# Both scatter-adds of an expert block issued together, with a set of padding rows for each

## The reference

```python
probs = softmax(xt @ Wr + br)
top_p, top_idx = top_k(probs, 2)
weights = top_p / top_p.sum(axis=-1, keepdims=True)
xn = (xt - mu) * rsqrt(var + 1e-5)
xe = xn[None] * ln_g[:, None] + ln_b[:, None]           # 8 experts
h = gelu(einsum('end,edh->enh', xe, W1) + b1)           # 256 -> 1024
y = einsum('enh,ehd->end', h, W2) + b2                  # 1024 -> 256
out = (weights[:, :, None] * y[top_idx]).sum(axis=1)    # added to x
```

## Time and profile before

| | us |
|---|---|
| median of 3 runs | 4400.84 |
| lowest, highest | 4399.68, 4402.47 |
| span of the profiled execution | 4400.9 |
| experts stage (about) | 3390 to 4400.9 |

### The profile page before, as it was taken

One profiled execution on the slowest core, in us unless ns is written; L12 is line 12 of the kernel. 1 busy time (PEld: TensorE's weight loads), 2 busy tenths in 40 slices (PEclk: granted clock), 3 DMA queues, 4 the chain that ended last, 5 costly groups with the idle time before them and its releaser, 6 DMA issues. The chain is left out here.

```text
span 4400.9 us, 84837 instructions
## 1 busy us (share of the span) xinstructions
PE 4086.7 (93%) x19450; PEld 3374.9 (77%) x19450; DVE 2987.8 (68%) x5419; ACT 2610.6 (59%) x8831; POOL 2599.1 (59%) x2378
## 2 busy tenths in 40 slices
PE   4999599999999999999999999999985888888887
PEld 3888488888888888888888888888985777777776
DVE  5666699999999999999999999997666000000000
ACT  1444587888788878887888787776232222222222
POOL 3444577777777777777777777775113233333332
PEclk8999799999999999999999999999967999999999
DMA  3333333443444333433443444433223455555554
GB/s 117 103 101 98 116 103 103 104 104 103 104 104 104 104 104 104 103 103 104 104 104 103 103 103 104 104 103 85 79 80 107 147 153 152 155 161 156 152 161 119
DMA packets 432067, 497.39 MB, mean 113 GB/s; under 512 B 253111, under 2 KB 343707, under 8 KB 417707
## 3 DMA queue, kind: packets, MB, share of 16 engines
q0 software_dynamic: 105984, 260.17, 22.1%
q1 hardware_dynamic: 326059, 236.92, 18.8%
HBM read 433.72 MB, written 63.07 MB: 113 GB/s over the span
## 5 line engine op out<-in xcount | busy, mean ns | idle before, releaser
L615 POOL DMA_INDIRECT k_x<-gather_table,edges_src x1760 | 1995.9, 1134 | 576.9 <-issue 446.4
L632 ACT ACTIVATE k_x<-k_x,edges_y 128x64 f32<-128x64 f32 x5280 | 1303.0, 335 | 4.9 <-DMA k_x<-gather_table,edges_src 4.9
L738 PE MATMUL edges_ps_sum<-k_x,edges_hot_y 128*128 128x256 f32 x3520 | 1094.2, 393 | 0.5 <-issue 0.5
L738 PE MATMUL edges_ps_sum<-k_x,edges_hot 128*128 128x256 f32 x3520 | 1048.1, 379 | 0.0
L639 ACT ACTIVATE edges_hot_y<-edges_hot,edges_y 128x128 f32<-128x128 f32 x1760 | 562.4, 390 | 506.9 <-DVE edges_hot L678 506.9
L727 PE MATMUL edges_ps_edge<-k_w_e,edges_hT 100*128 100x256 f32 x3520 | 836.4, 380 | 7.8 <-ACT edges_hT L625 7.8
L694 DVE TENSOR_TENSOR k_x<-k_x,edges_ps_edge 128x768 f32<-128x768 f32 x880 | 794.4, 941 | 0.0
L738 PEld LDWEIGHTS edges_ps_sum<-k_x,edges_hot_y 128*128 128x128 f32 x3520 | 633.6, 190 | 175.3 <-issue 107.1
L727 PEld LDWEIGHTS edges_ps_edge<-k_w_e,edges_hT 100*128 100x128 f32 x3520 | 670.8, 191 | 101.5 <-issue 7.6
L738 PEld LDWEIGHTS edges_ps_sum<-k_x,edges_hot 128*128 128x128 f32 x3520 | 670.0, 190 | 91.1
L1341 DVE TENSOR_TENSOR experts_raw<-experts_ps_y,experts_b 128x256 f32<-128x256 f32 x112 | 42.3, 419 | 908.7 <-PE experts_ps_y L1297 908.7
(11 more groups left out here) (233 smaller groups left out, 3996.6 us busy)
## 6 DMA issues: line engine op xcount, KB each, us to landing
experts_w<-in_w SPq DMA_DIRECT2D x112, 1024.0 KB
k_x<-gather_table,edges_src POOLq DMA_INDIRECT x1760
edges_el<-el_hi SPq DMA_DIRECT2D x880, 20.0 KB
edges_el<-el_lo SPq DMA_DIRECT2D x440, 20.0 KB
nodes_el<-in_el SPq DMA_DIRECT2D x46, 170.0 KB, 2.4
el_hi<-nodes_el_hi SPq DMA_DIRECT2D x46, 170.0 KB, 1.9
el_lo<-nodes_el_lo SPq DMA_DIRECT2D x46, 170.0 KB, 2.0
experts_b<-in_b SPq DMA_DIRECT2D x56, 128.0 KB
```

Of the source, the lines that this page charges most:

```text
L615: nc.gpsimd.indirect_dma_start(out=rows[k][:, j, :], out_offset=None, in_=K.table_d.rearrange("t p d -> (t p) d"), in_offset=bass.Indirect ...
L632: x = nc.scalar.activation(Z[k % 2][:, j, MUL * (i + 1):MUL * (i + 2)], rows[k][:, j, 0:MUL], ACT.Identity, scale=y[k][:, j, 1 + i:2 + i])
L738: x = t.matmul(into[:, :, o, :], rows_hot[k % 2][:, j, :], msg[k % 2][:, j, o * D:(o + 1) * D], start=j == 0 and o == 0, stop=j == GC - 1, ...
```

## The change

The second scatter-add of a block no longer waits for the first. Both wait once for the two of the block before. As both halves of one block can then be under way together, the halves get different padding rows: `spare` has two columns, N_PAD + 1 + p and N_PAD + 129 + p, and `out` and `tok_d` have one more tile of 128 zero rows, which SP writes in the update stage.

```diff
-            sp.dma_start(out[NT], K.zeros[:, 0:D]).then_inc(c["begun"], 16)
-            sp.dma_start(K.tok_d[NT], K.zeros[:, 0:D]).then_inc(c["begun"], 16)
+            for pad in (NT, NT + 1):
+                sp.dma_start(out[pad], K.zeros[:, 0:D]).then_inc(c["begun"], 16)
+                sp.dma_start(K.tok_d[pad], K.zeros[:, 0:D]).then_inc(c["begun"], 16)
...
-            sp.wait_ge(c["begun"], 48)
+            sp.wait_ge(c["begun"], 80)
...
-            done(v.tensor_scalar(empty[:, :], empty[:, :], spare[:, :], None, ALU.mult))
+            by_half = empty[:, :].rearrange("p (b s) -> p b s", s=2)
+            done(v.tensor_tensor(by_half, by_half, spare[:, :].unsqueeze(1).to_broadcast([P, C // 2, 2]), ALU.mult))
...
-            nc.gpsimd.iota(spare[:, :], [[0, 1]], base=N_PAD + 1, channel_multiplier=1, allow_small_or_imprecise_dtypes=True)
+            nc.gpsimd.iota(spare[:, :], [[P, 2]], base=N_PAD + 1, channel_multiplier=1, allow_small_or_imprecise_dtypes=True)
...
-            bounds = dict(bounds_check=N_PAD + P - 1)
+            bounds = dict(bounds_check=N_PAD + 2 * P - 1)
...
+                if not (isinstance(n, int) and n == 0):
+                    wait_apart(pool, c["passed"], (c["added"], n * 32))
                 for s in range(2):
-                    if not (isinstance(n, int) and n == 0 and s == 0):
-                        wait_apart(pool, c["passed"], (c["added"], n * 32 + 16 * s))
                     nc.gpsimd.indirect_dma_start(out=flat(out), out_offset=at(idx_out[k][:, s:s + 1]), in_=yb[k][:, s, :],
...
-        K.tok_d = dram("tokens", (NT + 1, P, D))
+        K.tok_d = dram("tokens", (NT + 2, P, D))
...
-    out = nc.dram_tensor("out", (NT + 1, P, D), f32, kind="ExternalOutput").ap()
+    out = nc.dram_tensor("out", (NT + 2, P, D), f32, kind="ExternalOutput").ap()
```

More of the change, by code:

```diff
@@ L1069, in dispatch @@
             ("hot_lo", P), ("hot_hi", C), ("hot_id", C), ("hot_w", C)))
-        pos_i, spare, empty = m.sb("pos_i", [P, G], i32), m.sb("spare", [P, 1]), m.sb("empty", [P, C])
+        pos_i, spare, empty = m.sb("pos_i", [P, G], i32), m.sb("spare", [P, 2]), m.sb("empty", [P, C])
         ps_token, ps_weight = m.ps("token"), m.ps("weight")
```

## The result

The changed kernel takes 4210.24 us (median of three runs, 4207.49 to 4215.28) against 4400.84 us; the ratio is 0.9568, with a 95% interval of 0.9551 to 0.9585. The forecast was 4218 us, from 4208 to 4262. The profiled execution is the slowest of the three, with a span of 4213.5 us.

The account below looks back on a forecast made before the run. PE, waiting for late gathers and then slowed by the lower clock, was taken to bound the kernel. 4400.9 less 179.7 (54 blocks from 17.648 to 14.32 us) less 3.6 at the end gave 4218 us, range 4208 to 4262.

Parts of the forecast that it names:

- What bounds the kernel: Experts stage: PE loses 124.7 us waiting for gathered rows and 58.5 us in matmuls at the lower clock behind waits.
- The gathers move up by 8.5 us: On POOL, the second scatter-add starts 1.9 us after the first, not 10.46, so all behind it moves up 8.5 us.
- L: Time of an expert's load, from DVE's end of a block to the release of ACT's shift; 11.36 us before.
- L grows to 12.2 us: Expert load beside more POOL traffic: L from 11.36 (lower bound) to 12.2 us; two periods 28.64 us.
- The nearest row: A load in the old trace with two gathers and one scatter-add beside it, L = 12.03 us.
- P: Period of one block in the experts stage, forecast to go from 17.648 to 14.32 us.
- The new single wait: POOL's wait for both landings of the block before: costs nothing, both down after 11 to 12 us, about 2 us cover.
- The end of the program: Last scatter-add starts 1.9 or 4.4 us behind the one before, not 6.68; saves 4.8 or 2.3 us, 3.6 taken.
- A: Rival: the expert's load takes the whole extra traffic, L = 13.09 us, period 14.77 us, 4242 us; chance 0.21.
- B: Rival: gathers queue behind two scatter-adds and land 6 us later, period 16.15 us, 4316 us; chance 0.07.
- D: Rival: POOL is held in the second issue until the first's rows are taken; time stays 4401 us; chance 0.04.
- C: Rival: the two scatter-adds slow each other, both down after 19.1 us, period 20.0 us, 4525 us; chance 0.04.

Follow-up runs that it names:

- e9: Kernel before, with 8 idle matmuls added on PE ahead of the turn that waits in every other block: 4349.5 us, ratio 0.9881.
- e1: Kernel before, with only POOL's order changed, the gather of block n+3 between block n's two scatter-adds: stage 785.2 us, ratio 0.9628 on the slow chip.
- e10: e1 run again on another chip: stage 784.6 us, whole 4221.9 us, ratio 0.9590.
- e2: Changed kernel with the wait between the two scatter-adds put back, leaving the padding rows, zeros and multiply new: 5015.6 us, ratio 0.9999.
- e7: Changed kernel with two of eight chunks of the second layer left out and b2 not loaded: 4116.0 us, ratio 0.9350.
- e6: Changed kernel with two of eight chunks of the second layer left out on PE: 4152.0 us, ratio 0.9433.
- e3: Changed kernel with POOL waiting for both scatter-add landings before each gather in the loop: stage 829.9 us, ratio 0.9746 on the slow chip.
- e11: e3 run again on another chip: stage 843.6 us, whole 4261.1 us, ratio 0.9676.

## Why the prediction was right

- **What bounds the kernel.** Confirmed part by part. The waits for gathered rows and the clock behind them were the whole loss: e9 gives 53 us for the clock alone, e1 and e10 give back all that the stage loses without touching the scatter-adds' waits, e2 gives nothing.
- **The gathers move up by 8.5 us.** Measured 13.17 - 4.63 = 8.54 us. PE's waits went from 124.7 us to 0.2.
- **L grows to 12.2 us.** This is the term that was off, to the safe side, and with it what bounds the period: I had two periods at 28.64 us, bound by the load; they are 28.53 us, bound by PE. L has a median of 11.44 us (11.32 in the load around the rows shown: DVE ends at 3805.22, the shift starts at 3816.54). Before, the loads of the blocks whose gathers were in time had 11.34. So it grew by 0.1 us, and its lower bound was the right end. The nearest row from which I took 12.2 us, L = 12.03, was not the load alone: the turn for that shift was late too and ended only 0.25 us ahead of it,

```profile
3693.98 0.89 PE L1276 MATMUL experts_ps_x<-k_ident,experts_x 128*128 128x128 f32 x4 [4.79 <-DMA experts_x<-tokens,experts_idx]
```

  and the load's last packet ended 0.53 us ahead of it, 0.37 where only the load is waited for. That is 0.16 us of the 12.03; why that load still took some 11.9 stays open. In the changed kernel, of POOL's 384 packets for two scatter-adds and two gathers none ran ahead of 3813, and 223 ran from 3816 to 3818, with the load's last work done at 3816.5:

```profile
q0 software_dynamic: 223, 0.37, 68.2%
```

  With P at 14.267 instead of 14.32 this is 2.9 us of the 4.1 us between the forecast gain of 183.3 us and the measured 187.4.
- **The new single wait costs nothing.** Right, with more cover than I gave it: no landing delays a first scatter-add in the stage, and the cover is 3.4 to 4.6 us, not 2. Both are down 10.1 to 11.0 us after the first one's issue, not 11 to 12.
- **The end of the program.** I took 3.6 us between 2.3 and 4.8; it was 4.2. The last scatter-add stands 2.64 us behind the one before it, so the gap of straight-line code comes back only in part:

```profile
4205.91 1.56 POOL L1253 DMA_INDIRECT out<-experts_y,experts_idx_out  x1 [10.10 <-DVE experts_y L1349]
4208.55 1.55 POOL L1253 DMA_INDIRECT out<-experts_y,experts_idx_out  x1 [1.08 <-issue]
```

- **The rivals.** A fell: L grew by 0.1 us and not by 1.73. Beside A stood the round-robin rule of the Trainium skill (DMA: Bandwidth & Descriptors, "Queues, rings and completion order"), by which a DMA engine serves the queues that have work in turn, a packet at a time. The trace does not contradict the rule: from 3813 to 3816 both queues were served, 161 packets of POOL's and 120 of SP's. It contradicts what I drew from it for this change, since POOL's queue got nothing for 6 us behind its issue and so had little of the load left to lengthen. B and D fell by POOL's rows and by PE's waits of 0.2 us. C needed both scatter-adds down no sooner than 16.7 us after the first's issue; in the changed kernel it took 11.0 us at most.
- The median is another 3.3 us under the profiled run's span, within what the three runs differ by. That the time lies 7.4 us under the forecast is for the rest the sum of these small terms, all on the same side. The mechanism was right in all but the load as the bound, and the range was cut close at its low end: the median lies 2 us inside it, and one of the three runs (4207.49 us) under 4208.

## What to carry to other kernels

Where an engine issues DMAs for two purposes from one queue, look at what stands behind a wait in that queue before looking at the waiting DMA itself: here the scatter-adds had time enough, and only the gathers behind them did not. Moving the gathers ahead of the wait gives the same gain in the steady state as making the wait go, and needs no extra rows; it costs 5.8 us at the end, and leaves the scatter-adds no cover against a shorter period. And count a wait of a nearly full PE with the lower clock that follows it: 4.62 us of waiting cost 6.8 us here.

## What the hardware showed that was not expected

- Beside a load of 2 MB, two scatter-adds issued 1.9 us apart were both down 10.1 to 11.0 us after the first's issue in the changed kernel, the second some 0.8 us behind the first; with nothing beside it, one took 3.7 to 3.8 us. The first landed when the load ended: its landing lies within 0.5 us of the release of ACT's shift in the changed kernel. With b2 loaded last (e8) it came 0.6 to 1.5 us ahead of that release.
- A broadcast load of 128 KB from 1 KB of HBM, which seemed to hold the engines for 1.9 us, lengthened the load by 0.9 us when it was doubled (e5), and shortened it by 1.9 us when it was left out (e7 beside e6) and by 0.7 us when it was moved to the end (e8).
- The same kernel took 5017 us on one chip and 4401 us on others. The trace from the slow chip is that of e2, whose whole time is the same: its difference lies ahead of the experts stage, where PE waited 320.6 us for ACT in the edges stage and 7.8 us on the fast one, while the experts stage took 966.8 and 967.1 us. Why the chips differ stays open. The stages of e1 and e10 agree to a tenth of a per cent across the two chips, where the whole times of one kernel on the slow one spread over 1.4%; those of e3 and e11 are 1.7% apart.
